# An order written by hand in a five-engine kernel: x prepared one tile ahead, products with C inside the burst of silu, the maximum of h later

## What is computed

```python
# per batch b, inner channel d (512), state n (16), position l
dA    = exp(dt[b, d, l] * A[d, n])
state = state * dA + (dt * u)[b, d, l] * B[b, n, l]       # a scan over l
y     = sum_n state * C[b, n, l] + D[d] * u[b, d, l]
x     = x + tanh(g_x) * swap(y * silu(layernorm(x)))
# feed-forward, per position
h     = silu(bitlinear(layernorm(x), w_gate)) * bitlinear(layernorm(x), w_up)
out   = x + tanh(g_f) * bitlinear(h, w_down)
# bitlinear: rmsnorm, scale by 127 / max|.|, round; weights rounded to -1, 0, 1
```

## Time and profile before

| | |
|---|---|
| median of 3 runs | 668.48 us (667.66 to 670.59) |
| profiled execution, its own time | 668.09 us |
| its span, first to last instruction | 666.3 us |
| units 0 to 3 (76.1 to 182.0) | 105.9 us |
| units 4 to 15, to the last scan (181.99 to 588.24) | 406.25 us |
| behind the last scan's start | 78.1 us |
| lengths of units 4 to 15, us | 32.67, 34.57, 33.97, 33.97, 33.97, 33.97, 33.97, 35.20, 33.97, 34.95, 33.98, 31.06 (to its last scan only) |

### The profile page before, as it was taken

The page is one execution under the profiler, slowest core; times in us unless marked ns, Lnnn a source line. Parts: engine busy times, 40 slices in busy tenths (PEclk is TensorE's granted clock), DMA queues, the critical chain, the costliest instruction groups (busy, mean ns, idle before and its releaser), DMA issues. The chain is left out here.

```text
span 666.3 us, 9019 instructions
## 1 busy us (share of the span) xinstructions
PE 512.8 (77%) x2966; PEld 348.2 (52%) x2966; DVE 571.1 (86%) x781; ACT 507.9 (76%) x709; POOL 516.5 (78%) x297
## 2 busy tenths in 40 slices
PE   6998576766768686868696959596869786988996
PEld 2443365654655654645454646364646554654453
DVE  2889999999997989898989898989898998975543
ACT  4978699787968687878687868676867686867774
POOL 2444899999999898989898989897989898821000
PEclk9998777988859699999999999989998899899999
DMA  8994811613810100136311100282101010000000
GB/s 308 398 383 131 319 33 35 250 48 107 320 47 1 47 2 31 32 139 241 95 32 32 33 32 33 56 321 97 33 25 38 1 48 2 14 19 1 17 27 38
DMA packets 29985, 64.47 MB, mean 97 GB/s; under 512 B 3681, under 2 KB 11873, under 8 KB 26866
## 3 DMA queue, kind: packets, MB, share of 16 engines
q1 hardware_dynamic: 29938, 63.89, 27.0%
HBM read 55.75 MB, written 8.13 MB: 96 GB/s over the span
## 5 line engine op out<-in xcount | busy, mean ns | idle before, releaser
L667 POOL TENSOR_TENSOR area_s<-area_s,b_bc 128x1024 f32<-128x1024 f32 x128 | 300.5, 2362 | 30.2 <-DVE u_all L1143 25.6
L417 PE MATMUL pY<-ident,area_s 128*128 128x128 f32 x640 | 108.4, 297 | 121.4 <-DVE area_s L1151 120.3
L417 PEld LDWEIGHTS pY<-ident,area_s 128*128 128x128 f32 x640 | 75.1, 149 | 157.6 <-DVE area_s L1151 106.7
L868 ACT ACTIVATE pA<-dt_all,a_neg 128x512 f32<-128x512 f32 x160 | 108.2, 683 | 37.0 <-DVE area_s L1143 21.0
L1143 DVE TENSOR_TENSOR_SCAN area_s<-pA,area_s 128x512 f32<-128x512 f32 x96 | 114.7, 1209 | 10.8 <-ACT pA L868 9.4
L457 PE MATMUL pG<-wq_gu,area_f 128*128 128x512 fp8e4 x448 | 105.0, 379 | 3.3 <-ACT area_f L834 3.3
L659 POOL TENSOR_TENSOR u_all<-u_all 128x1024 f32<-128x1024 f32 x44 | 104.0, 2363 | 0.0
L1151 DVE TENSOR_TENSOR area_s<-area_s,pC 128x512 f32<-128x512 f32 x144 | 95.2, 663 | 4.3 <-DVE area_s L1143 3.9
L411 PE MATMUL pC<-ident,xdT 128*128 128x128 f32 x576 | 94.7, 294 | 0.7 <-ACT dt_all L765 0.7
L411 PEld LDWEIGHTS pC<-ident,xdT 128*128 128x128 f32 x576 | 75.3, 150 | 3.8 <-ACT dt_all L765 1.5
L497 PE MATMUL pT<-wq_dn,area_f 128*128 128x512 fp8e4 x256 | 67.2, 392 | 1.4 <-ACT area_f L859 1.4
(11 more groups left out here) (154 smaller groups left out, 952.3 us busy)
## 6 DMA issues: line engine op xcount, KB each, us to landing
b_bc<-bc_rows SPq DMA_DIRECT2D x16, 1024.0 KB, 8.2
area_s<-x SPq DMA_DIRECT2D x32, 256.0 KB, 2.9
u_all<-bc_rows SPq DMA_DIRECT2D x14, 512.0 KB, 5.8
b_bc<-w_gate SPq DMA_DIRECT2D x1, 4096.0 KB, 14.7
dt_all<-x SPq DMA_DIRECT2D x1, 4096.0 KB, 25.0
area_f<-w_up SPq DMA_DIRECT2D x1, 4096.0 KB, 34.4
area_f<-w_down SPq DMA_DIRECT2D x1, 4096.0 KB, 14.7
out<-area_f SPq DMA_DIRECT2D x16, 256.0 KB, 2.1
```

Of the source, the lines that this page charges most:

```text
L417: mm = pe.matmul(pY[:, k * P:(k + 1) * P], src[:, k * P:(k + 1) * P], ident[:, :], is_transpose=True, start=(first and k == 0), stop=(last ...
L667: gp.tensor_tensor(db[c % NDB], du[s % 2].rearrange("p (a l) -> p a l", a=1).to_broadcast([P, CH, L]), b_bc[:, CH * c:CH * c + CH, :], ALU ...
L868: act.activation(exp_bank(s, n), dt_all[:, s, :], ACT.Exp, scale=a_neg[:, s % NT, n:n + 1]).then_inc(S["s_exp"], 1)
```

## The change

It moves work and adds none; the numbers of instructions stay as they are.

- The products with C of own states 7 and 10 go from steps 9 and 11 of DVE to steps 11 and 12. On PE, `y_sum` of state 7 goes behind gates 0 and 1, and gates 2 and 3 ahead of `y_sum` of state 10.
- x one tile ahead: in a first unit both t1 and t1+1 are prepared (`stats` at steps 4 and 8, `x_scales` at 7 and 13), in a middle unit t1+1 alone (`stats` at 4, `x_scales` at 13), in a last unit none. `normalise` of t1+1 stands at step 10 of ACT, just ahead of the exponential of step 13, and `scale_x` and `copy_xqT` of a middle or last unit at steps 2 and 4, with `xq_transpose` ahead of those of h.
- `gated_y` goes from step 1 to 2, `h_max` from 0 to 3, `h_scales` from 3 to 4, `output` from 12 to 13; `scale_h` and `copy_hqT` one step later; `skip` (ACT) from 2 to 1, and its sum on PE (`y_skip`) far up.
- On PE, `c_bcast` of state 2 goes ahead of all `down` parts, which now stand together, and the broadcasts and sums of states 3 and 6 ahead of the transposes of h.

```diff
-C_STEP = {2: 3, 3: 5, 6: 7, 7: 9, 10: 11, 11: 13, 14: 15, 15: 16}
+C_STEP = {2: 3, 3: 5, 6: 7, 7: 11, 10: 12, 11: 13, 14: 15, 15: 16}
...
                 c_bcast(s, 3)
-                if t3 >= 0:
-                    down(t3, 3, s)
-                if t2 >= 0:
-                    hq_transpose(t2, 0, pG)
-                    hq_transpose(t2, 1, pG)
-                y_sum(s, 3)
-                y_sum_pooled(s, 0)
-                c_bcast(s, 6)
+                y_skip(s)
                 if t3 >= 0:
                     down(t3, 4, s)
+                    down(t3, 5, s)
+                if t1 % NT:
+                    pe.wait_ge(S["f_h"], FC * t1)
+                    xq_transpose(t1, pG[0])
+                y_sum(s, 3)
+                c_bcast(s, 6)
+                y_sum_pooled(s, 0)
                 if t2 >= 0:
-                    hq_transpose(t2, 2, pG)
-                    hq_transpose(t2, 3, pG)
...
-                    if n == 2:
+                    if n == 1:
                         skip(s)
-                    if n in (4, 5) and t2 >= 0:
-                        scale_h(t2, n - 4)
-                    if n == 5:
+                    if n == (2 if t1 % NT else 8):
+                        scale_x(t1)
+                    if n == (4 if t1 % NT else 9):
+                        copy_xqT(t1, pG[0][:, :])
+                    if n in (5, 6) and t2 >= 0:
+                        scale_h(t2, n - 5)
+                    if n == 6 and t1 % NT == 0:
                         normalise(t1)
...
+                    if n == 10 and (t1 + 1) % NT:
+                        normalise(t1 + 1)
...
-                    if n == 0 and t2 >= 0:
-                        h_max(t2)
-                    if n == 1:
+                    if n == 2:
                         gated_y(s - 1)
                     if n == 3 and t2 >= 0:
+                        h_max(t2)
+                    if n == 4 and t2 >= 0:
                         h_scales(t2)
```

More of the change, by code:

```diff
@@ L525, in _ @@
                     y_sum_pooled(s - 1, 3)
-                if t3 >= 0:
-                    down(t3, 0, s)
                 c_bcast(s, 2)
                 if t3 >= 0:
-                    down(t3, 1, s)
-                    down(t3, 2, s)
+                    for part in range(4):
+                        down(t3, part, s)
                 y_sum(s, 2)
                 c_bcast(s, 3)
-                if t3 >= 0:
-                    down(t3, 3, s)
-                if t2 >= 0:
-                    hq_transpose(t2, 0, pG)
-                    hq_transpose(t2, 1, pG)
-                y_sum(s, 3)
-                y_sum_pooled(s, 0)
-                c_bcast(s, 6)
+                y_skip(s)
                 if t3 >= 0:
                     down(t3, 4, s)
+                    down(t3, 5, s)
[5 more added lines that the diff above has]
+                y_sum_pooled(s, 0)
                 if t2 >= 0:
-                    hq_transpose(t2, 2, pG)
-                    hq_transpose(t2, 3, pG)
-                if t3 >= 0:
-                    down(t3, 5, s)
+                    if t1 % NT:
+                        pe.wait_ge(S["f_xqT"], t1 + 1)
+                    for r in range(HR):
+                        hq_transpose(t2, r, pG)
                 y_sum(s, 6)
                 c_bcast(s, 7)
[L551 to L557, removed]
+                if t1 % NT == 0:
+                    past(pe, S["f_h"], FC * t1)
+                    past(pe, S["f_hqT"], HR * t1 - 1)
+                    xq_transpose(t1, pG[0])
                 gate(t1, 0)
                 gate(t1, 1)
+                y_sum_pooled(s, 1)
+                y_sum(s, 7)
+                c_bcast(s, 10)
+                gate(t1, 2)
+                gate(t1, 3)
                 y_sum(s, 10)
                 c_bcast(s, 11)
-                gate(t1, 2)
-                gate(t1, 3)
                 up(t1, 0)
@@ L705, in _ @@
                 times_c(s, 0)
-                x_rstd(t1)
                 times_b(s, NDB + 1)
+                if t1 % NT == 0:
+                    x_rstd(t1)
                 times_b(s, NDB + 2)
+                if t1 % NT and (t1 + 1) % NT:
+                    x_rstd(t1 + 1)
                 times_c(s, 1)
+                if t1 % NT == 0:
+                    x_rstd(t1 + 1)
                 times_b(s, NDB + 3)
@@ L1177, in _ @@
                         times_c(s - 1, 15)
+                    if n == 13 and t3 >= 0:
+                        output(t3)
                     for state, step in C_STEP.items():
@@ L1180, in _ @@
                             times_c(s, state)
-                    if n == 0 and t2 >= 0:
-                        h_max(t2)
-                    if n == 1:
+                    if n == 2:
                         gated_y(s - 1)
                     if n == 3 and t2 >= 0:
+                        h_max(t2)
+                    if n == 4 and t2 >= 0:
                         h_scales(t2)
-                    if n == 4:
+                    if n == 4 and t1 % NT == 0:
                         stats(t1)
-                    if n == 6:
+                    if n == 7 and t1 % NT == 0:
                         x_scales(t1)
-                    if n == 12 and t3 >= 0:
-                        output(t3)
+                    if n == (4 if t1 % NT else 8) and (t1 + 1) % NT:
+                        stats(t1 + 1)
+                    if n == 13 and (t1 + 1) % NT:
+                        x_scales(t1 + 1)
                     if n in (13, 14, 15):
```

10 lines of the change are left out of this document (3 added, 7 removed).

## The result

The changed kernel takes 662.25 us (median of 4 runs, 660.1 to 663.32) against 669.38 for the kernel before (4 runs): ratio 0.9895, 95% interval 0.9865 to 0.9924. It is 1.05% faster; the forecast was 657.4, or 1.6%. The profiled execution, the shortest of the four, took 660.1 us with a span of 658.3. Units 4 to 15 take 398.8 us of it (395.5 forecast, 406.25 before), what lies ahead of them and what lies behind are each within 0.6 us of before.

A forecast was written before the change was run, and what follows sets the result against it. Bound: a loop of DVE's scans releasing exponentials and ACT's burst holding them back. Units 4 to 15 take 383.5 us at full clock plus 12.0 for the clock, 395.5, 10.7 below before; 668.09 - 10.7 = 657.4 us, range 647 to 667.

The forecast's parts named there:

- The bound: Units 4 to 15: DVE's scans release exponentials and ACT's burst holds them back; scan 11 to scan 14 took 8.49 us.
- Units at full clock: Changed unit lengths without clock falls: first 34.3 us, middle 32.4, last 30.35, against 33.97 before.
- the distance from scan 11 to scan 14: DVE's stretch across ACT's burst in a middle unit: 8.57 us instead of 8.49, with 1.66 us more work done.
- The clock: PE idles ahead of state 3's sum, 4.0 to 4.5 us in first and middle units, and its clock falls to half.
- The charge of 12.0 us: Loss to low PE clock over units 4 to 15, added to 383.5 us at full clock to give 395.5.
- the 22.7 us saved at full clock: Units 4 to 15 without the clock's charge: 383.5 us against 406.25 before.
- the price of a fall: Late h transposes at half clock: 1.2 us in nine units, nearest to unit 11 before, 0.4 in three last ones.
- The parts moved at no cost: Moves of gated_y, skip and output, costed at nothing because their readers come over 1 us later.
- POOL level with DVE: POOL's 31.87 us a unit as next bound: 129.2 us over four units against DVE's 129.45, no gain beyond.
- Full clock (645.4): Rival, chance 0.17 (full clock or nearly so): falls don't come or cost nothing; 645.4 us for the kernel.
- the burst would take 1.5 us a unit more than counted: Rival, chance 0.13: state 11's broadcast and normalise replace the removed waits in the burst; 666 us, no change.
- A low clock for 7 us and more: Rival "slower", chance 0.06: low clock behind each long idle stretch also covers gates 2 and 3; 5.1 us in nine units, 691.

The follow-up runs named there:

- e8: Changed kernel plus two groups of h transposes moved ahead of state 3's sum, filler matmuls, and state 10's sum and state 11's broadcast ahead of gates 2 and 3: 0.9965.
- e1_fill: Changed kernel with 28 unread matmuls (20 in last units) in PE's idle stretch ahead of the sum of state 3: 648.33 us, ratio 0.9674 to the kernel before.
- e7: Control: kernel before with 20 unread matmuls in its own PE idle stretch ahead of the sum of state 2: 668.75 us, ratio 0.9996.
- e3: Kernel before with only the products of states 7 and 10 at steps 11 and 12 and PE's gates reordered to match: 654.02 us, ratio 0.9754.
- e6: e3 with 20 unread matmuls in its PE idle stretch ahead of the sum of state 2: 652.03 us, ratio 0.9766 to the kernel before.
- e11: Changed kernel with h_max back at step 0, gated_y at 1, h_scales at 3 and scale_h at 4 and 5: 658.47 us, ratio 0.9834 to the kernel before.
- e9: e2_h01 with x_scales ahead of step 13's product and a first unit's second stats at step 6: 642.49 us, ratio 0.9611 to the kernel before.
- e2_h01: Changed kernel with the first two groups of h transposes moved on PE ahead of the sum of state 3: 646.0 us, ratio 0.9634 to the kernel before.

## Why the prediction was right, and where it was off

**The bound.** Right: the loop through DVE's scans and ACT's burst. e8 shows it from the other side, as 1.46 us of wait inside the burst turn into a unit over 1 us longer.

**Units at full clock.** 34.3, 32.4 and 30.35 forecast, 34.12, 32.55 and 30.34 in e1_fill. The terms of a middle unit hold as well: scan 11 at 19.16 (19.2 forecast), the product of state 11 waiting 1.00 us, `times_up` and silu without a wait. Only the distance from scan 11 to scan 14 is 0.2 longer, 8.77 instead of 8.57.

**The clock.** The mechanism was right. The idle stretch was forecast as 4.0 to 4.5 us in first and middle units and 3.0 in last ones, and was 3.8 to 4.7 (2.8 in unit 9) and 2.80. From unit 6 on all six stretches of 3.8 us and more had a fall of the clock in them or right behind, and of the four of 2.8 us two had. The Trainium skill (TensorE: Matmul & The Clock Gate, HAM oscillation) says that gaps between groups of matmuls throttle the engine; the changed kernel agrees for these six, and e7 shows that a long gap isn't needed.

The charge of 12.0 us was too low. Over e1's lengths at full clock, unit 5 is 3.0 us longer, with 10.24 us at half clock, the four middle units with a fall behind the stretch (33.77, 34.17, 34.07 and 34.24) 1.2 to 1.7, 1.5 in the mean, the first units 8 and 12 1.3 each, unit 9 0.4, and the last units 7, 11 and 15 1.3, 0 and 1.6 (unit 15 is 29.05, in e1 27.43). That is 15.0 us; unit 4, 32.14 long with a slow stretch, is not above its forecast. The 3.0 us over the charge are nearly all of the 3.3 by which the loop missed the forecast, and two thirds of the 22.7 us saved at full clock, not half, are lost. From the 660.1 of the profiled execution to the median of 662.25 are another 2.2 us, the spread of the runs. Some errors cancelled: units 4 and 9 were charged 1.2 each and cost 0 and 0.4.

**The step that was mis-sized** is the price of a fall, 1.2 us in nine units and 0.4 in the last ones. Where it is paid differs by unit. In unit 10 scan 11 comes 1.29 us later than in e1 (20.45 against 19.16), behind the late copies of h, and the burst takes 0.34 more. In unit 8 scan 11 is on time at 21.27 and all is lost in the burst, 9.56 us against 8.22, where the product of state 10 waits for its broadcast. The traces also show that the price goes by where in the unit the slow stretch lies. In units 6 to 15 of the kernel before, e3 and e7, the eleven of 3.41 us that begin 2 or 8 to 10 us into a unit cost nothing. The two that begin at 13.4 and 14.3, both in unit 11, have a unit 1.15 and 1.23 us longer, and of this some 0.35 is not the clock's: e6, at full clock throughout, has a unit 11 of 33.08 where its others are 32.73. In the changed kernel eight of nine from unit 6 on begin at 11.4 to 14.5 and cost 1.2 to 1.7, last units included. So unit 11 of before was the nearest row for the place, but a fall there cost an estimated 0.8 to 0.9 us (1.15 and 1.23 less 0.35), which would mean that the changed order made it dearer and that 1.2 came as near as it did by luck. Why it was dearer was not tested.

**The parts moved at no cost.** The place of `gated_y` with `h_max` was right as a whole, but its effect wasn't seen: the late maximum brings the transposes of x forward. I had put its worth in POOL's wait, which e11 shows to be slack.

**POOL level with DVE.** Half right. POOL wasn't the bound in any kernel here: the only waits of DVE for POOL in all these loops are two of 0.30 us in e3. A unit of 31.51 us in e9 is below the 31.87 that I took as POOL's floor, though POOL is busy 31.33 of it.

**Rivals.** Full clock (645.4) is what e1_fill came near to, with 648.3. That the burst would take 1.5 us a unit more than counted didn't come, as e1's units are within 0.2 us of the working; the price set on it was also wrong in itself, for 1.5 us in twelve units are 18 us and not 9, and it would have given 675. A low clock for 7 us and more came in unit 5 alone (10.24 us in two stretches of 3.41 and 6.83, 3 us lost).

**What stays open.** Whether a stretch of 2.8 or 2.9 us is followed by a fall differs from unit to unit, in the kernel before too, and unit 14 of before and four units of e7 had falls without a long stretch. The runs show what a fall costs and where, not a rule for when it comes. The spread of the changed kernel's runs (660.1 to 663.3) may be the same thing; only one of them has a trace.

## What to carry to other kernels

When an order is written by hand around a burst on one engine, ask of every instruction in the burst what its producer is queued behind: gates behind a sum that waits for a third engine cost 17.5 us here. An edit that gathers PE's free work at one place also gathers its idleness; look at what stands behind the gap, and put real work with slack into it (transposes of h, 2.6% gained on the changed kernel) before thinking of filler. And undo each part of a change of many parts: here one part alone brought 2.5%, the whole 1.05%, and the whole with two groups of transposes moved back 3.7%.

## What the runs showed of the hardware that I had not expected

Twenty-eight matmuls more in a unit, with results that nobody reads, made the kernel 2.2% faster (e1 against the changed kernel), because the granted clock was 1.00 instead of 0.95 in most units; 20 of them in each unit of the kernel before brought 0.9996, with 2.0 us gained in the loop and 2.5 lost behind it. A stretch at half clock of 3.41 us cost 0 to 1.7 us, by what stood in it: nothing in units 12, 14 and 15 of before, 1.5 in middle units of the changed kernel, at most 1.1 in e2_h01 from unit 6 on. And falls came without an idle stretch of over 2 us (e7, four units).
